# LSTM loop of a graph and attention kernel: output gates in PSUM banks of their own, another order of gate tiles, other filler matmuls on TensorE

## The reference, cut to what matters

```
def step(carry, xp):
    h, c = carry
    gates = xp + h @ W_hh.T
    i, f, g, o = jnp.split(gates, 4, axis=-1)
    c = sigmoid(f) * c + sigmoid(i) * tanh(g)
    h = sigmoid(o) * tanh(c)
    return ((h, c), h)
_, hs = jax.lax.scan(step, (h0, c0), x_proj)
```

## Time and profile before

| | us |
|---|---|
| median of 3 runs | 18018.25 (18016.04 to 18020.35) |
| the profiled execution | 18005.85 |
| its span, first to last instruction | 18003.9 |
| LSTM loop in it, first gate weight load to the last step | from 6047 to 17656 |
| mean granted TensorE clock over the span | 0.927 |

### The profile page before, as it was taken

One profiled execution on the slowest core, in us unless ns is written; L12 is line 12 of the kernel. 1 busy time (PEld: TensorE's weight loads), 2 busy tenths in 40 slices (PEclk: granted clock), 3 DMA queues, 4 the chain that ended last, 5 costly groups with the idle time before them and its releaser, 6 DMA issues. The chain is left out here.

```text
span 18003.9 us, 1832831 instructions
## 1 busy us (share of the span) xinstructions
PE 14961.4 (83%) x837380; PEld 13287.0 (74%) x837380; DVE 7375.8 (41%) x47174; ACT 6807.2 (38%) x36128; POOL 2722.7 (15%) x4549
## 2 busy tenths in 40 slices
PE   2367576767311999999999999999999999999994
PEld 1356465655201899999999999999999999999993
DVE  2465656556334333333333333333333333333335
ACT  1244353535211244444444444444444444444441
POOL 0165463726310000000000000000000000000000
PEclk9978788888655999999999999999999999999996
DMA  0143352424311100000000000000000000000000
GB/s 22 40 126 116 90 154 62 145 70 135 117 56 37 49 2 2 2 2 2 2 2 2 2 2 2 2 2 2 2 2 2 2 2 2 2 2 2 2 2 15
DMA packets 720915, 580.96 MB, mean 32 GB/s; under 512 B 579762, under 2 KB 631100, under 8 KB 708536
## 3 DMA queue, kind: packets, MB, share of 16 engines
q1 hardware_dynamic: 482385, 316.90, 6.1%
q0 software_dynamic: 238400, 262.61, 5.6%
HBM read 325.17 MB, written 252.12 MB: 32 GB/s over the span
## 5 line engine op out<-in xcount | busy, mean ns | idle before, releaser
L1342 PE MATMUL p_g<-ring,wh 128*32 128x32 f32 x800000 | 8266.6, 197 | 2.3 <-issue 2.3
L1342 PEld LDWEIGHTS p_g<-ring,wh 128*32 128x32 f32 x800000 | 7571.2, 108 | 801.2 <-DVE ring L1437 414.8
L1431 DVE CUSTOM_DVE_ANT_1 cj<-cell 128x4 f32<-128x4 f32 x12500 | 2037.8, 163 | 6796.8 <-ACT cell L1384 6796.8
L1384 ACT ACTIVATE cell<-p_g 128x3 f32<-128x3 f32 x12500 | 2172.9, 174 | 6691.9 <-PE p_g L1342 6691.9
L1320 PE MATMUL p_g<-xq,idn 128*128 128x6 f32 (+2 forms) x15006 | 2495.7, 262 | 13.4 <-PEq L1330 13.4
L1387 ACT ACTIVATE tc<-cell 128x1 f32<-128x1 f32 x12500 | 2482.3, 199 | 0.0
L1437 DVE SCALAR_TENSOR_TENSOR ring<-og,tc 128x1 f32<-128x1 f32 x12500 | 1924.0, 159 | 755.9 <-ACT og L1395 1.5
L1466 POOL COPY hist<-ring 128x6 f32 x2501 | 475.6, 190 | 11569.2 <-POOLq L1465 11569.2
L1320 PEld LDWEIGHTS p_g<-xq,idn 128*128 128x128 f32 x15006 | 2049.0, 189 | 218.6 <-issue 13.6
L297 POOL DMA_INDIRECT eb<-node_tab,eidx x1650 | 2059.0, 1248 | 627.4 <-issue 446.1
L1325 PE MATMUL p_f<-wh,idn 128*128 128x128 f32 (+1 forms) x7500 | 2043.6, 354 | 0.0
(11 more groups left out here) (205 smaller groups left out, 8154.4 us busy)
## 6 DMA issues: line engine op xcount, KB each, us to landing
edge_tab<-eb SPq DMA_DIRECT2D x96, 1391.1 KB
edge_tab<-eb SPq DMA_DIRECT2D x96, 758.8 KB
eb<-node_tab,eidx POOLq DMA_INDIRECT x1650
xp_tab<-xo SPq DMA_DIRECT2D x50, 500.0 KB, 2.6
xq<-xp_tab SPq DMA_DIRECT2D x1251, 8.0 KB, 1.7
xq<-xp_tab SPq DMA_DIRECT2D x1250, 12.0 KB, 1.7
x<-w_in SPq DMA_DIRECT2D x8, 1024.0 KB
node_tab<-hrow SPq DMA_DIRECT2D x50, 126.0 KB
```

The source lines that it names most:

```text
L1342: m = pe.matmul(to[32 * q:32 * q + 32], wh[:, k, D * q + 32 * c:D * q + 32 * c + 32], ring[:, (s - 1) % TS, k:k + 1].broadcast_to([128, W] ...
L1384: act.activation(cell[:, s, k, 0:6:2], gate_at(h, u, k)[:, :, 0], ACT.Tanh).then_inc(l_s[k], 1)
L1431: dve.tensor_tensor_reduce(cj[:, k, :].rearrange("p (a b) -> p a b", a=2), cell[:, s, k, 0:4].rearrange("p (a b) -> p a b", a=2), cell[:, ...
```

## The change

The output gates of the two halves get a PSUM bank, a semaphore and a ScalarE instruction each (before: one for both). The bank of `fill` goes; all eight banks are now `p_g`. TensorE does tile 4 with half 0 before it waits for half 1, tile 5 (k = 0) after the first signal, and 6 with both halves, signal, 7 with both halves, signal. The last `gate` call before each of the first two signals has 1 column in place of 32. `place_x` writes 16 columns for each gate value in place of one: 144 columns (to h = 1) or 96 (to h = 0) in each of its two calls at u = 0, 48 or 32 in each of its two calls at u = 1. `fill` is gone at u = 1; at u = 2 it is two rounds of four matmuls of 96 columns in form 128*32, into unread columns of a `p_g` bank. ScalarE's order becomes gates(0), gates(1), output gate 0, tanh_c(0), output gate 1, tanh_c(1), and `new_h(k)` waits for tanh_c(k).

```diff
-                part_of = ((0, 3), (3, 6), (6, 8))
-                p_g = [[ps(sub, f"p_g{h}{n}") for n in range(3)] for h in range(2)]
-                p_f = ps(sub, "p_f")
+                part_of = ((0, 3), (3, 6), (6, 7), (7, 8))
+                p_g = [[ps(sub, f"p_g{h}{n}") for n in range(4)] for h in range(2)]
...
-                        return pe.matmul(p_g[h][n][:, 0:HB[h] * (c1 - c0) * W].rearrange("p (t c w) -> p t c w", c=c1 - c0, w=W)[:, :, :, 0],
-                                         idn[:], xq[h][:, :, c0:c1],
+                        to = p_g[h][n][:, 0:HB[h] * (c1 - c0) * W].rearrange("p (t c w) -> p t c w", c=c1 - c0, w=W)
+                        return pe.matmul(to[:, :, :, 0:W // 2], idn[:], xq[h][:, :, c0:c1].unsqueeze(3).broadcast_to([128, HB[h], c1 - c0, W // 2]),
                                          start=True, stop=False, skip_group_check=True)
...
-                    def fill(cols):
-                        return pe.matmul(p_f[:, 0:cols], idn[:], wh[:, 0, 0:cols], start=True, stop=True, skip_group_check=True)
+                    def fill(h):
+                        for q in range(4):
+                            pe.matmul(p_g[h][3][32 * q:32 * q + 32, 384:480], wh[:, 0, 32 * q:32 * q + 32], wh[:, 0, 0:96],
+                                      start=False, stop=True, skip_group_check=True)
...
                             pe.wait_ge(l_h[0], s + 1)
-                            for c in (0, 1, 2, 3):
+                            for c in (0, 1, 2, 3, 4):
                                 gate(c, 0)
                             pe.wait_ge(l_h[1], s + 1)
-                            for c in (0, 1, 2):
-                                m = gate(c, 1)
-                            m.then_inc(l_g[0], 1)
-                            for c in (4, 5):
-                                gate(c, 0)
-                            for c in (3, 4, 5):
-                                m = gate(c, 1)
-                            m.then_inc(l_g[1], 1)
+                            gate(0, 1)
+                            gate(1, 1)
+                            gate(2, 1, 1).then_inc(l_g[0], 1)
+                            gate(5, 0)
+                            gate(3, 1)
+                            gate(4, 1)
+                            gate(5, 1, 1).then_inc(l_g[1], 1)
                             for k in range(KC):
-                                for c in (6, 7):
-                                    m = gate(c, k)
-                            m.then_inc(l_g[2], 1)
+                                gate(6 + k, 0)
+                                gate(6 + k, 1).then_inc(l_g[2 + k], 1)
...
                             elif u == 1:
-                                place_x(1 - h, 2).then_inc(l_xf[1 - h], 1)
-                                fill(128)
+                                place_x(1 - h, 2)
+                                place_x(1 - h, 3).then_inc(l_xf[1 - h], 1)
                             else:
-                                fill(256)
+                                fill(1 - h)
+                                fill(1 - h)
...
+                            act.wait_ge(l_g[2], s + 1)
+                            out_gate(0)
                             act.wait_ge(l_c[0], s + 1)
-                            tanh_c(0)
-                            act.wait_ge(l_g[2], s + 1)
-                            act.activation(og[:, (s % 2), :], gate_at(h, u, 2)[:, :, 0], ACT.Tanh).then_inc(l_o, 1)
+                            tanh_c(0).then_inc(l_tc[0], 1)
+                            act.wait_ge(l_g[3], s + 1)
+                            out_gate(1)
                             act.wait_ge(l_c[1], s + 1)
-                            tanh_c(1).then_inc(l_tc, 1)
+                            tanh_c(1).then_inc(l_tc[1], 1)
...
-                            dve.wait_ge(l_o, s + 1)
-                            new_h(0)
-                            dve.wait_ge(l_tc, s + 1)
-                            new_h(1)
+                            for k in range(KC):
+                                dve.wait_ge(l_tc[k], s + 1)
+                                new_h(k)
```

More of the change, by code:

```diff
@@ L1264, in gps_kernel @@
                 cj = sb(sub, "cj", [128, KC, 4])
-                part_of = ((0, 3), (3, 6), (6, 8))
-                p_g = [[ps(sub, f"p_g{h}{n}") for n in range(3)] for h in range(2)]
-                p_f = ps(sub, "p_f")
+                part_of = ((0, 3), (3, 6), (6, 7), (7, 8))
+                p_g = [[ps(sub, f"p_g{h}{n}") for n in range(4)] for h in range(2)]
                 l_in, l_z, l_go, l_pe = sem("l_in"), sem("l_z"), sem("l_go"), sem("l_pe")
                 l_x, l_xf = [sem("l_x0"), sem("l_x1")], [sem("l_xf0"), sem("l_xf1")]
-                l_g = [sem(f"l_g{n}") for n in range(3)]
-                l_o = sem("l_o")
+                l_g = [sem(f"l_g{n}") for n in range(4)]
                 l_s, l_c, l_h = ([sem(f"l_{n}{k}") for k in range(KC)] for n in ("s", "c", "h"))
-                l_tc = sem("l_tc")
+                l_tc = [sem("l_tc0"), sem("l_tc1")]
                 l_hist, l_half = sem("l_hist"), sem("l_half")
@@ L1330, in _ @@
                     pe.sem_inc(l_x[0], -16)
-                    for n in range(3):
+                    for n in range(4):
                         m = place_x(0, n)
@@ L1336, in _, with gate @@
                             h, u = place(s)
-                            def gate(c, k):
-                                n = min(c // 3, 2)
-                                to = gate_at(h, u, n)[:, c - 3 * n, :]
+                            def gate(c, k, w=W):
+                                n = c // 3 if c < 6 else c - 4
+                                to = gate_at(h, u, n)[:, c - part_of[n][0], 0:w]
                                 for q in range(4):
@@ L1343, in gate @@
                                                   wh[:, k, D * q + 32 * c:D * q + 32 * c + 32],
-                                                  ring[:, (s - 1) % TS, k:k + 1].broadcast_to([128, W]), start=False, stop=(k == KC - 1), skip_group_check=True)
+                                                  ring[:, (s - 1) % TS, k:k + 1].broadcast_to([128, w]), start=False, stop=(k == KC - 1), skip_group_check=True)
                                 return m
                             pe.wait_ge(l_h[0], s + 1)
-                            for c in (0, 1, 2, 3):
+                            for c in (0, 1, 2, 3, 4):
                                 gate(c, 0)
                             pe.wait_ge(l_h[1], s + 1)
-                            for c in (0, 1, 2):
-                                m = gate(c, 1)
-                            m.then_inc(l_g[0], 1)
-                            for c in (4, 5):
-                                gate(c, 0)
-                            for c in (3, 4, 5):
-                                m = gate(c, 1)
-                            m.then_inc(l_g[1], 1)
+                            gate(0, 1)
[5 more added lines that the diff above has]
+                            gate(5, 1, 1).then_inc(l_g[1], 1)
                             for k in range(KC):
-                                for c in (6, 7):
-                                    m = gate(c, k)
-                            m.then_inc(l_g[2], 1)
+                                gate(6 + k, 0)
+                                gate(6 + k, 1).then_inc(l_g[2 + k], 1)
                             if u == 0:
@@ L1387, in tanh_c, with out_gate @@
                                 return act.activation(tc[:, (s % 2), k:k + 1], cell[:, (s + 1) % TS, k, 5:6], ACT.Tanh)
+                            def out_gate(k):
+                                act.activation(og[:, (s % 2), k:k + 1], gate_at(h, u, 2 + k)[:, :, 0], ACT.Tanh)
                             act.wait_ge(l_g[0], s + 1)
@@ L1391, in _ @@
                             gates(1)
+                            act.wait_ge(l_g[2], s + 1)
+                            out_gate(0)
                             act.wait_ge(l_c[0], s + 1)
-                            tanh_c(0)
-                            act.wait_ge(l_g[2], s + 1)
-                            act.activation(og[:, (s % 2), :], gate_at(h, u, 2)[:, :, 0], ACT.Tanh).then_inc(l_o, 1)
+                            tanh_c(0).then_inc(l_tc[0], 1)
+                            act.wait_ge(l_g[3], s + 1)
+                            out_gate(1)
                             act.wait_ge(l_c[1], s + 1)
-                            tanh_c(1).then_inc(l_tc, 1)
-                        for q in (l_g[0], l_g[1], l_g[2], l_c[0], l_c[1]):
+                            tanh_c(1).then_inc(l_tc[1], 1)
+                        for q in (l_g[0], l_g[1], l_g[2], l_g[3], l_c[0], l_c[1]):
                             act.sem_inc(q, -TS)
@@ L1445, in _ @@
                                 dve.sem_inc(l_half, -1)
-                            dve.wait_ge(l_o, s + 1)
-                            new_h(0)
-                            dve.wait_ge(l_tc, s + 1)
```

(6 more changed lines are left out.)

## The result

The changed kernel takes 18103.62 us (median of 5, 18088.6 to 18110.5), the one before 18018.25 (18012.44 to 18023.39): ratio 1.0046, 95% interval 1.0031 to 1.006. So it is slower by 0.46%, 85 us, where 1.0%, 177 us, was forecast. The sign and the mechanism stand; one term of the sum, that of s4, was too large. The profiled execution took 18088.6 us with a span of 18086.8, 82.9 more than before.

A forecast was written before the change was run, and what follows sets the result against it. The prediction took the chain to bound s0 and s2, and the fill s1, s3 and s4. +0.13 - 0.06 + 0.06 - 0.07 + 0.09, about +0.14 us a body, times 1250 is +175 us: 18195 us, range 17900 to 18405.

The forecast's parts named there:

- s4: Last of the loop body's five steps, with two rounds of fill: 1.97 us, was 1.88, +0.09 (from -0.01 to +0.26).
- The chain: Within a step, last gate tile, output gates, new_h(0), then TensorE: 1.76 us in place of 1.81.
- s0: First step of the loop body, preload calls of 144 columns: 1.94 us, was 1.81, +0.13.
- s2: Third step of the loop body, preload calls of 96 columns: 1.87 us, was 1.81, +0.06.
- s1: Second step of the loop body, preload calls of 48 columns, no fill: 1.83 us, was 1.89, -0.06.
- s3: Fourth step of the loop body, preload calls of 32 columns, no fill: 1.82 us, was 1.89, -0.07.
- The model of the 128-wide work: TensorE's preloads and fills: a pass takes the larger of 0.11 us and 0.84 ns a column; leaving the form 0.10.
- the turn: Loop end on TensorE's sequencer, from its first semaphore operation to the next step: 0.77 us if all is needed.
- rival A: At the loop's end: the turn costs nothing, s4 ends by the chain at 1.76 us; 17930 us, chance 0.10.
- B: In s0 to s3: wide preloads cost no more than narrow ones, 1.79 us each; 17830 us, chance 0.09.
- C: TensorE's clock falls: a tenth of the loop at 0.50 gives +625 us, 18800; chance given as "C and D 0.05".
- D: Code loading: the longer loop body doesn't stay loaded, about 2 us a body, above 20000 us; "C and D 0.05".

The follow-up runs named there:

- E9: The kernel before the change without its fills, all else as it was: 17694.3 us, ratio 0.9822.
- E4: The changed kernel with preloads of one column for each gate value, the fill of s4 kept: 17800.4 us.
- E10: The changed kernel with one-column preloads, each call done as four matmuls of 32 output partitions, and no fill: 17434.56 us, ratio 0.9676.
- E1: The changed kernel without its two rounds of fill in s4: 17930.02 us.
- E3: The changed kernel with three rounds of fill in s4 in place of two: 18211.64 us.
- E6: The changed kernel with one semaphore operation more at the end of TensorE's loop body: 18286.68 us.
- E7: The kernel before the change with one semaphore operation more at the end of TensorE's loop body: 18074.29 us.
- E5: The changed kernel with preloads of one column for each gate value and no fill: 17587.79 us, ratio 0.9762.
- E12: E10 with the last gate call before each of the first two signals back at 32 columns: 17431.86 us, ratio 0.9678.
- E13: E10 with ScalarE's tanh_c(0) before output gate 0, and new_h(0) waiting for the latter: 17217.06 us, ratio 0.9557.

## Why the prediction was wrong, and where it was right

- *What bounds the kernel.* Right. The chain through the output gates ended s0 and s2, the fills ended s1, s3 and s4. E9 shows the latter: without fills all five steps are 1.80 to 1.81. (One reading in it is wrong and changes nothing: TensorE's clock row stands at 9 from the 14th slice on, not from the 16th.)
- *The model of the 128-wide work* (a pass takes the larger of 0.11 for its weights and 0.84 ns a column, and 0.10 for leaving the form). Right to 0.01 us in s0, s1, s2 and s3 of the changed kernel, and in E4.
- *The chain.* Right: `new_h(0)` at 1.55 gives 1.76, hidden in the changed kernel, in the open in E10. The second `new_h` isn't over well before the next step in s0, as was said, but 0.04 before it (7932.20 + 0.35 against 7932.59); it holds nothing up, since its result is needed five `gate` calls into the next step.
- *s4: this is the step that failed.* "The chain from that operation to the next step is 0.77 (1.11 to 1.88), and the branch alone ends at 1.75. So s4 takes 1.87 if nothing had to follow the branch, and 2.00 if all 0.77 is needed; I take 1.97, nearer the measured chain." The sum of the forecast had +0.09 for s4; it measured +0.01 (1.88 to 1.89). The mechanism, the sequencer's issue of 32 fill instructions and then its turn, was right (E1, E3, E6). The size of the turn was not: it is 0.665 and not 0.74 to 0.77. The other 0.10 was not part of it, since the old fill of 256 columns, with its 0.10 to leave the form, ended s4 at 1.88, where the turn could have ended it at 1.108 + 0.665 = 1.77 (1.80 with the 0.03 of its branch). E7 shows the 0.10 of slack: one more operation of 0.155 raises s4 by 0.05 only. The forecast had this very reading in its rival A (the old fill alone explains 1.88), and should have asked what the row then says of the turn: only that it is at most 0.77. In the trace it had 0.13 between the branch's end and the next step; after the change this distance is 0.055. The other 0.03 of the difference lies before the branch, in the 0.127 that became 0.097. So s4 came out near its lower bound of 1.87. That its issue term of 0.12 fitted is partly luck, as E1 and E3 show.
- *The sum.* The body went from 9.279 to 9.341 us on average, +0.062, x 1250 = +77 us. Another 6 us are from before the loop, which starts at 6053.3 in place of 6047.4. Together they are the +83 between the spans; between the medians it is +85. The forecast's +0.14 less its error of 0.08 in s4 is the same +0.06.
- *Rival A* (the turn costs nothing, s4 at 1.76) is wrong: with the fill s4 is 1.89, and one operation more in the turn adds all of its 0.15 (E6). *B* is wrong (E4). *C*: the clock was 1.00 in the loop, and even with no filler it is, after the start (E5, E9, E10). *D*: nothing of it in the trace.
- *The short columns.* The forecast gave them up to 0.03 us on a signal that nobody waits for. They are not on the path (E12), and they didn't even move the signal, see below.

## What to carry to other kernels

A distance in a trace at whose end other work ends too is an upper bound of what it costs, and not its cost (here 0.77 us, of which 0.665 were needed). When a change takes that other work away, take as the lower bound the parts that are seen to follow one another, and test it by adding one operation, once with and once without the other work. Filler work that nobody reads still costs issue time on its sequencer (here 0.16 us for 32 instructions) and, in another form, the switch on its engine (0.10 us), so put it where a wait is sure and long, and first try the kernel without it. And before a chain is shortened, list what else ends at almost the same time (here the chain at 1.81 us and the narrow preload at 1.79): the gain is at most the distance to the next one.

## What the runs showed of the hardware that was not expected

- A matmul of 1 column signals no sooner than one of 32. Its record is shorter (171 ns against 198 on average in E10, by form), but ScalarE's first tanh starts 0.80 us after the step's start in most steps of both E10 and E12, and the second at 1.10 in both. So the end of a matmul's record doesn't tell when it signals; the start of the engine that waits does. The Trainium skill, TensorEngine Tiling (Array Packing), Instruction Overhead, says that a matmul with one free column has the same latency as one with 60, and this agrees.
- ScalarE starts `tanh_c(0)` 0.07 us after the instruction before it where that is a one-column or three-column read of PSUM (changed kernel, kernel before). From a tanh of one column from SBUF to the output gate behind it it was 0.11 in E13 and 0.09 in E10 (`tanh_c(0)` to output gate 1). What makes the difference between the two is open.
- At clock 0.50 the loop's start lasted 20 us in the kernel before, 86 in E5 and 198 in E4, although TensorE was busy nearly without a break in E4, and 24 to 25 in E9, E10 and E12, which have no filler. Which work shortens it is open.
